# RWKV attention and mixture of experts on one core: VectorE's attention program reordered, ScalarE's scaled output moved

## The reference

```
xk = x * mix_k + shifted * (1 - mix_k)          # xv, xr alike; shifted: one token back
k, v, r = xk @ Wk.T, xv @ Wv.T, xr @ Wr.T
# scan over the tokens, per channel:
out = (e1 * num + e2 * v) / (e1 * den + e2)     # mx + w and k give the exponents
num, den, mx = e1s * num + e2s * v, e1s * den + e2s, max(mx + w, k)
y = (sigmoid(r) * out) @ Wo.T
x = x + layernorm(y)
```

## Time and profile before

| | before |
|---|---|
| median of the runs | 1229.62 us |
| span of the profiled execution | 1230.5 us |
| TensorE matmuls busy | 1125.4 us (91%) |
| VectorE busy | 868.8 us (71%) |
| ScalarE busy | 727.4 us (59%) |
| GpSimd busy | 300.0 us (24%) |

### The profile page before, as it was taken

One profiled execution on the slowest core, in us unless ns is written; L12 is line 12 of the kernel. 1 busy time (PEld: TensorE's weight loads), 2 busy tenths in 40 slices (PEclk: granted clock), 3 DMA queues, 4 the chain that ended last, 5 costly groups with the idle time before them and its releaser, 6 DMA issues.

```text
span 1230.5 us, 15805 instructions
## 1 busy us (share of the span) xinstructions
PE 1125.4 (91%) x5208; PEld 811.8 (66%) x5208; DVE 868.8 (71%) x1984; ACT 727.4 (59%) x1250; POOL 300.0 (24%) x264
## 2 busy tenths in 40 slices
PE   5988999999999986889999889999998999999894
PEld 3635455454545444668888778888887887878761
DVE  4699999999999989599888844544454444444385
ACT  2666779788888888733332245665565555546353
POOL 2010202122020101100000035424433453434246
PEclk9999999999999987889999999999999999999898
DMA  8401033150303225765452079979988988887799
GB/s 318 177 7 35 5 99 78 60 137 34 103 35 69 77 61 171 169 233 193 148 201 81 5 232 260 250 238 250 255 229 255 254 239 250 230 228 181 185 319 354
DMA packets 79538, 206.23 MB, mean 168 GB/s; under 512 B 10209, under 2 KB 10337, under 8 KB 76641
## 3 DMA queue, kind: packets, MB, share of 16 engines
q1 hardware_dynamic: 59424, 156.98, 36.3%
q0 software_dynamic: 20032, 48.24, 20.5%
HBM read 145.93 MB, written 59.28 MB: 167 GB/s over the span
## 4 chain that ended last, share of the span: by engine, by line
PE 33%; DMA 11%; DVE 8%; issue 3%; POOL 2%; ACT 2%; POOLq 0%; DVEq 0%; ACTq 0%
DMA ysh<-k_sb,mixf 8%; PE bank L713 6%; PE bank L688 3%; PE bank L690 3%; PE bank L689 3%; PE bank L670 3%; PE bank L672 3%; PE bank L671 3%; DMA xres<-h,mixf 2%; PE bank L728 2%; PE bank L702 2%; PE bank L729 2%; PE bank L730 1%; DVE stats L1879 1%; PE bank L524 1%
## 5 line engine op out<-in xcount | busy, mean ns | idle before, releaser
L577 PE MATMUL bank<-mix_ring,weights 128*128 128x512 f32 x512 | 224.4, 595 | 2.8 <-ACT k_sb L829 2.8
L577 PEld LDWEIGHTS bank<-mix_ring,weights 128*128 128x128 f32 x512 | 97.6, 191 | 123.2 <-issue 118.2
L1338 POOL DMA_INDIRECT ysh<-k_sb,mixf x64 | 113.5, 1773 | 201.9 <-DMA ysh<-k_sb,mixf 108.3
L584 PE MATMUL bank<-weights,rw 128*128 128x512 f32 x256 | 119.0, 621 | 9.9 <-DVE rw L1491 5.5
L1100 ACT ACTIVATE k_sb<-bank 128x512 f32<-128x512 f32 x64 | 38.2, 597 | 143.9 <-PE bank L672 140.5
L1796 DVE TENSOR_TENSOR run_max<-run_max 128x256 f32<-128x256 f32 x64 | 27.3, 426 | 117.4 <-ACT e_split L1136 117.4
L1314 POOL DMA_INDIRECT xres<-h,mixf x48 | 53.6, 1117 | 221.0 <-DVE mixf L1782 210.3
L670 PE MATMUL bank<-h_high,ffn_w 128*128 128x512 f32 x256 | 103.3, 403 | 2.7 <-ACT k_sb L1100 2.7
L688 PE MATMUL bank<-ffn_w,s_split 128*128 128x512 f32 x256 | 102.5, 401 | 1.8 <-DVE s_split L1775 1.8
L1802 DVE TENSOR_TENSOR wkv_split<-wkv,xnd_split 128x1024 fp32r<-128x1024 f32 x48 | 58.9, 1227 | 61.8 <-ACT xnd_split L1144 61.8
L671 PE MATMUL bank<-h_low,ffn_w 128*128 128x512 f32 x256 | 101.1, 395 | 0.0
(11 more groups left out here) (244 smaller groups left out, 2550.9 us busy)
## 6 DMA issues: line engine op xcount, KB each, us to landing
wkv<-in_w SPq DMA_DIRECT2D x96, 512.0 KB
state<-in_w SPq DMA_DIRECT2D x32, 512.0 KB
xin<-h SPq DMA_DIRECT2D x8, 1024.0 KB, 6.7
xin<-in_x SPq DMA_DIRECT2D x7, 1024.0 KB, 7.3
xres<-in_x POOLq DMA_DIRECT2D x7, 1024.0 KB, 9.4
x<-xres SPq DMA_DIRECT2D x7, 1024.0 KB, 4.8
h<-hb SPq DMA_DIRECT2D x7, 1024.0 KB, 4.5
ht<-xnT SPq DMA_DIRECT2D x7, 1024.0 KB, 8.7
```

The lines of the kernel that those rows point to most:

```text
L577: mm = pe.matmul(bank[:, d, :], W(j)[:, ck, d * P:(d + 1) * P], mix_slot(4 * j + ck), start=(ck == 0), stop=(ck == CK - 1))
L584: mm = pe.matmul(bank[:, s, :], rw[:, ck, s * P:(s + 1) * P], W(3)[:, ck, :], start=(ck == 0), stop=(ck == CK - 1))
L1338: pool.indirect_dma_start(t["ysh"], bass.IndirectOffsetOnAxis(ap=scatter_token[:, e % IB:e % IB + 1], axis=0), e_out[q], None, compute_op= ...
```

## The change

No operation of the attention is added or removed; the order changes on two engines.

VectorE. `moments`, `gaps`, `scans` and `refine` are cut into parts: `row_stats` and `row_moments`; `gap_scan` and `gap_taken`; `scans` (up to the numerator's scan), `num_added` (L1474) and `num_gated` (L1477); `recip_used` (L1484, L1486) and `refined` (L1491). `scans_then_gaps` weaves the gap of the following chunk into the end of the scans. In a period the parts are put so that another operation stands between a producer and its consumer: a mix between `recip_used` and `refined`, a mix between `bn_stats` and `bn_aggr`, the diffs one step ahead of the mixes. The gap of chunk c+1 thereby moves ahead of two operations of chunk c. Where there are no mixes any more (the last tiles), `recip_used` and `refined` stay adjacent.

ScalarE. In the middle of the period, `y_scaled` of tile tau-1 is moved ahead of `ln1_normalise`, and with it the order of the rest: before `r_round(0)`, `ln1_normalise`, `r_round(1)`, `carry_over`, `seed`, `exps(2)`, `y_scaled`; after `carry_over`, `seed`, `r_round(0)`, `exps(2)`, `y_scaled`, `r_round(1)`, `ln1_normalise`.

```diff
@@ ScalarE, period @@
+                    carry_over(tau, 1)
+                    seed(tau, 3)
                     if ahead:
                         r_round(tau + 1, 0)
-                    if has(tau, 2):
-                        ln1_normalise(tau + 2)
-                    if ahead:
-                        r_round(tau + 1, 1)
-                    carry_over(tau, 1)
-                    seed(tau, 3)
                     exps(tau, 2)
                     if behind:
                         y_scaled(odd, tau - 1)
+                    if ahead:
+                        r_round(tau + 1, 1)
+                    if has(tau, 2):
+                        ln1_normalise(tau + 2)
                     if ahead:
                         r_round(tau + 1, 2)
                     recip(tau, 2)
@@ VectorE, new helper @@
+            def scans_then_gaps(tau, c, *following):
+
+                scans(tau, c)
+                if following:
+                    gap_scan(*following)
+                num_added(tau, c)
+                if following:
+                    gap_taken(*following)
+                num_gated(tau, c)
@@ VectorE, ahead of the periods @@
+            gap_scan(0, 0, 0)
             mix(0, RJ, 0)
-            gaps(0, 0, 0)
+            gap_taken(0, 0, 0)
...
             shift(1, 1)
+            for ck in range(CK):
+                diff(1, ck)
             for ck in range(CK - 1):
-                diff(1, ck)
                 mix(1, KJ, ck)
-            diff(1, CK - 1)
@@ VectorE, period @@
                 if behind:
-                    refine(tau - 1, 3)
+                    recip_used(tau - 1, 3)
+                if here:
+                    mixes(KJ, 3)
+                if behind:
+                    refined(tau - 1, 3)
...
-                    mixes(KJ, 3)
-                    scans(tau, par, 0)
+                    scans_then_gaps(tau, 0, tau, par, 1)
                     mixes(VJ, 0, 1)
-                    gaps(tau, par, 1)
+                    recip_used(tau, 0)
                     mixes(VJ, 2)
-                    refine(tau, 0)
+                    refined(tau, 0)
                     if has(tau, 2):
-                        ln1_moments(tau + 2)
+                        ln1_stats(tau + 2)
                     mixes(VJ, 3)
+                    if has(tau, 2):
+                        row_moments(1, tau + 2)
                     if last(tau):
                         ffn_rest(0, 0)
-                    scans(tau, par, 1)
-                    mixes(RJ, 0)
-                    gaps(tau, par, 2)
+                    scans_then_gaps(tau, 1, tau, par, 2)
...
-                    mixes(RJ, 1)
-                    refine(tau, 1)
-                    if ahead:
-                        r_rest(tau + 1, 0)
-                        r_rest(tau + 1, 1)
-                    mixes(RJ, 2, 3)
+                    mixes(RJ, 0, 1)
+                    recip_used(tau, 1)
+                    mixes(RJ, 2)
+                    refined(tau, 1)
+                    rests(0, 1)
+                    mixes(RJ, 3)
...
-                    scans(tau, par, 2)
-                    gaps(tau, par, 3)
-                    if ahead:
-                        r_rest(tau + 1, 2)
-                    if has(tau, 2):
-                        diff(tau + 2, 0)
-                        mix(tau + 2, KJ, 0)
-                    refine(tau, 2)
-                    if ahead:
-                        r_rest(tau + 1, 3)
-                    if has(tau, 2):
-                        diff(tau + 2, 1)
-                        mix(tau + 2, KJ, 1)
+                    scans_then_gaps(tau, 2, tau, par, 3)
+                    rests(2)
+                    diffs_next(0)
+                    recip_used(tau, 2)
+                    diffs_next(1)
+                    refined(tau, 2)
+                    mixes_next(KJ, 0)
+                    rests(3)
+                    mixes_next(KJ, 1)
...
-                    scans(tau, par, 3)
-                    if has(tau, 2):
-                        diff(tau + 2, 2)
-                        mix(tau + 2, KJ, 2)
                     if ahead:
-                        gaps(tau + 1, 1 - par, 0)
-                    if has(tau, 2):
-                        diff(tau + 2, CK - 1)
+                        scans_then_gaps(tau, 3, tau + 1, 1 - par, 0)
+                    else:
+                        scans_then_gaps(tau, 3)
+                    diffs_next(2, CK - 1)
+                    mixes_next(KJ, 2)
```

More of the change, by code:

```diff
@@ L1408, in ln1_moments @@
                     dve.wait_ge(S["x_loaded"], 16 * (tau + 1))
-                moments(1, xin, tau)
+                row_stats(1, xin, tau)
+            def ln1_moments(tau):
+                ln1_stats(tau)
+                row_moments(1, tau)
             def shift(tau, par):
@@ L1452, in gaps, with gap_taken, scans @@
                                        max_col[:, b, 0:1], ALU.add, ALU.max).then_inc(S["max_scanned"], 1)
+            def gap_taken(tau, par, c):
+                b = c % 2
+                u = 4 * tau + c
                 dve.wait_ge(S["max_scanned"], u + 1)
                 dve.tensor_tensor(unit[:, b, G, :], k_sb[:, par, c, :], max_col[:, b, 0:TT], ALU.subtract).then_inc(S["gap_ready"], 1)
-            def scans(tau, par, c):
+            def scans(tau, c):
                 b = c % 2
@@ L1471, in scans, with num_added @@
                                        ALU.mult, ALU.add).then_inc(S["scanned"], 1)
+            def num_added(tau, c):
+                b = c % 2
+                u = 4 * tau + c
                 dve.wait_ge(S["r_times_v"], u + 1)
@@ L1474, in scans, with num_gated @@
                 dve.tensor_tensor(unit[:, b, NUM, :], unit[:, b, NUM, :], sums_of[:, b, 0, 0:TT], ALU.add).then_inc(S["num_ready"], 1)
+            def num_gated(tau, c):
+                b = c % 2
+                u = 4 * tau + c
                 dve.wait_ge(S["num_ready"], u + 1)
@@ L1486, in refine, with refined @@
                 dve.tensor_tensor(unit[:, b, NUM, :], unit[:, b, NUM, :], unit[:, b, G, :], ALU.mult).then_inc(S["a_ready"], 1)
+            def refined(tau, c):
+                b = c % 2
+                u = 4 * tau + c
                 dve.wait_ge(S["resid_ready"], u + 1)
@@ L1495, in ln3 @@
                 dve.wait_ge(S["x1_summed"], 16 * (tau + 1))
-                moments(3, x1_of(tau), tau)
+                row_stats(3, x1_of(tau), tau)
+                row_moments(3, tau)
             def routing_constants():
@@ L1701, in mixes, with mixes_next, diffs_next, rests @@
                             mix(tau + 1, j, ck)
-                if behind:
-                    refine(tau - 1, 3)
+                def mixes_next(j, *chunks):
+                    if has(tau, 2):
+                        for ck in chunks:
+                            mix(tau + 2, j, ck)
+                def diffs_next(*chunks):
+                    if has(tau, 2):
+                        for ck in chunks:
+                            diff(tau + 2, ck)
+                def rests(*chunks):
+                    if ahead:
+                        for ck in chunks:
+                            r_rest(tau + 1, ck)
+                if behind:
+                    recip_used(tau - 1, 3)
[3 more added lines that the diff above has]
+                    refined(tau - 1, 3)
                 if behind_all(tau):
```

9 lines of the change are left out of this document (5 added, 4 removed).

## The result

The changed kernel takes 1237.19 us (median of 20 runs), the kernel before 1230.45 us in the same comparison: ratio 1.0053, 95% interval 1.0034 to 1.0073, that is 4 to 9 us slower. The profiled execution spans 1235.8 us against 1230.5. The forecast was 1233.7 us, with 1228 to 1243 as its range. As a change it was +4.1 us, at the lower end of the measured 4 to 9.

What follows compares the result with a forecast made beforehand. VectorE's program was taken to set the period, ScalarE's exponentials just behind, TensorE nearly full. Terms -1.5 + 3.75 + 3.1 - 1.4, with +0.1 for TensorE's later outputs, gave +4.1 us: 1233.7 us, range 1228 to 1243.

Steps and rivals of the forecast that it cites:

- part 3: VectorE at r_rest(1) stands still 3.25 us: ScalarE's r_round(1) is ready after 7.65 us, VectorE arrives after 4.4.
- Leg B: From the start of scans of chunk 1 to that of chunk 2: forecast 16.41 us, +2.23 on average.
- part 1: Operations pulled away from their producers start without idle: VectorE's own work falls by 2.9 us a period.
- legs A and C: From scans of chunk 0 to chunk 1, and of chunk 2 to chunk 3: forecast -0.82 and -0.85 us.
- leg D: From scans of chunk 3 to chunk 0 of the next period: does not shorten, forecast +0.19 us.
- pulling apart saves nothing: Rival: VectorE's cost is the same wherever the producer stands, +18 us in all, 1247 us; chance 0.04.
- A full period: One of periods 1 to 5, four legs summed: forecast +0.75 us, bounds +0.4 to +1.1, five of them +3.75.
- Prologue and period 0: The attention's start, up to chunk 0 of period 1: four diff pairs ahead and the legs, together -1.5 us.
- Period 6: Tile with no layer norm ahead, its chain starting from TensorE: 53.9 against 50.76 us, +3.1, bounds +0.75 and +4.
- a rival for it: TensorE's clock falls behind pauses of 2.4 us ahead of the transposes: +10 us on top, 1243 us; chance 0.08.
- a sign that I had set down as one of being wrong: A granted TensorE clock below 1.00 in full periods would show the forecast wrong.
- Period 7: Last tile, without r work: four gains 0.2 + 0.3 + 0.4 + 0.5 = -1.4 us, bounds 0 and 3.5.

Runs made afterwards that it cites:

- after_again: The changed kernel run once more, not a line different; only its trace up to rw was read: period 6 took 55.18 us.
- act_alone: ScalarE's changed order alone, with VectorE's program of the kernel before; ratio to the kernel before 1.0137.
- rest1_late: The changed kernel with VectorE taking r_rest(tau+1, 1) behind chunk 2's scans, gap and gate; 1222.9 us, ratio to the kernel before 0.9954.
- order_alone: The kernel before with only ScalarE reordered: carry_over, seed, r_round(0), r_round(1), exps(2), y_scaled, ln1_normalise; ratio to the kernel before 1.0010.
- ve_alone: VectorE's changed program alone, with ScalarE's order of the kernel before; ratio to the kernel before 1.0034.
- pauses_p7: rest1_late plus three VectorE waits for its own last result in the last tile's first leg (chunk 0); ratio to the kernel before 0.9938.

## Why the prediction was right, and where it was not

- **The new wait** (part 3): forecast 3.25 us, measured 3.27 in period 3, 3.28 on average. Leg B forecast 16.41, measured 16.45; over the five full periods it grew by 2.26, forecast 2.23. Taking it away on either engine brought the time below that of the kernel before, so the decisive step stands by experiment.
- **The pairs** (part 1): legs A and C 14.27 and 12.68 against forecasts of 14.35 and 12.76; leg D 12.92 for 12.96. The rival "pulling apart saves nothing" is out.
- **A full period**: +0.67 us on average, forecast +0.75. TensorE's wait ahead of the transposes, put at 2.4 us, was 1.7 on average.
- **Prologue and period 0**: -1.27 and -1.42, forecast -1.5 together. Chunk 0 of period 0 starts at 58.4 to 59.6 us in the kernels with the new VectorE program and at 59.3 to 60.1 in those with the old one, so part of the first is scatter.
- **Period 6**: +4.57, forecast +3.1, above my upper bound of +4. The mechanism was right, but the clock was missing. I had a rival for it (TensorE's pause ahead of the transposes makes the clock fall) and gave it little because the pauses would be 2.4 us at most and one of 2.84 us in period 0 had cost nothing. It did happen, in two places out of five in each trace of the changed kernel, where the pauses were 1.93 and 2.3 us. Most of it was hidden in the changed kernel's first trace (after_again lost 1.1 us in period 4); where ScalarE's chain starts from TensorE, in period 6, it cost 1.5 us instead of the 10 of that rival. The failing step is to have treated it as all or nothing. With it came a sign that I had set down as one of being wrong: a granted clock of 0.99 in the full periods.
- **Period 7**: +1.48, forecast -1.4, outside my bounds of 0 and 3.5 us of gain. This step failed. I read ScalarE's work there and not what GpSimd does between it: legs B and C did shorten, by 0.42 and 0.48, but leg A grew by 2.27 because `ln3_normalise` waited for L1257. All four terms of my sum were gains, and none had GpSimd in it; a gap scan and four TENSOR_TENSORs in a row beside GpSimd made leg A a loss. The mechanism was in no rival.
- **The stretch behind rw**: -1.4 us in this pair of traces, forecast unchanged. The other traces scatter from 731 to 749 us behind rw, so this says nothing. That a shift of rw reaches the total one for one holds in most kernels as far as the runs can tell (act_alone rw +18.0, total +14 to +20; rest1_late -6.9, -3 to -8), but not in order_alone (+4.5, total -1.5 to +3.9) and ve_alone (+0.6, total +1.0 to +7.4).
- **The sum** came out near by chance in part: errors of +1.5 (period 6), +2.9 (period 7) and -1.7 (all ahead of period 6) make +2.6 or so on rw, and the -1.4 behind it brings the span to 1235.8 for 1234.6. The median is 3.5 us off, because I carried a distance of 0.9 us from the span of one execution to the median of others. In all executions on record the time is 1.7 to 1.9 us above their own span; that the median before lay below the span only means that the profiled execution was longer than most. 1237.19 lies in the stated range, but above the forecast's own 1231.5 to 1236.

## What to carry to other kernels

When instructions are reordered on one engine, list what its neighbour asks for and when: here 3.3 us of one small operation, 7.6 us deep in ScalarE's queue where VectorE wanted it after 4.4, undid in every period what other legs gained (0.9 us each in A and C), and moving that operation, or its user on VectorE, turned a loss of 0.5% into a gain of 0.45%. Look then at who works beside the reordered engine: here a GpSimd operation on 4 columns, and an exp that stood behind it. And a wait that is taken away gives back only the distance to the next chain, here 1.5 of 3.3 us.

## What the hardware showed that was not expected

- The same GpSimd operation of 128 x 4 elements takes 0.42, 0.94 or 2.15 us, by the order of VectorE's operations beside it: it ends 0.06 us behind the end of a TENSOR_TENSOR that has a mix, a scan or a pause behind it. A pause of 0.04 us is enough (0.61 us). Its group from 100 to 490 us, before and changed (five of 0.94 us, one of 2.15):

```profile
L1257 POOL TENSOR_TENSOR offset<-neg_mean,rstd 128x4 f32<-128x4 f32 x6 | 2.5, 416 | 0.5
```

```profile
L1257 POOL TENSOR_TENSOR offset<-neg_mean,rstd 128x4 f32<-128x4 f32 x6 | 6.8, 1140 | 0.5
```

- TensorE's clock behind a pause, over periods 1 to 5 of all traces: the 16 transposes took 1.93 to 2.03 us behind every pause up to 1.62 us. Behind six pauses of 1.93 to 1.98 us they took 2.02 or 2.03 us four times, and 3.29 and 3.56. Behind 2.07 to 2.17 us they took 2.03, 2.48, 2.86 and 2.96, and behind all nine of 2.32 to 3.19 us 2.67 to 3.65. In period 0 it came out otherwise: behind 2.85, 2.85 and 2.89 us they took 2.03 us, behind 2.88 us 3.39. Pauses of nearly the same length don't always give the same clock.
- The Trainium skill, "VectorE: DVE Perf Modes", section "The DRAIN you can't avoid", says that a semaphore between two VectorE operations costs nothing extra. The traces of this kernel disagree: with an operation between producer and user, legs A and C are 0.9 us shorter with the same operations in them (15.17 to 14.27, 13.61 to 12.68), and the idle of 2.1, 2.0, 0.7 and 0.7 us ahead of the moved groups is 0.0. The three waits that pauses_p7 adds say the same: from the gap's scan to the operation behind the gate VectorE takes 3.36 us instead of 2.96, 0.13 us for each wait on the operation directly ahead.
